# Six-tap gather and three-tap dense sampling: position rows broadcast by DMA through DRAM, the second corner sum moved to TensorE, V projected earlier

## What is computed

```python
feat = relu(norm_or_bias(conv1x1(x)))              # 64 channels, 32 x 32
off  = conv3x3(feat, w_off)                        # per pixel and tap: dy, dx (and a mask for b = 0)
py, px = y + ky + dy, x + kx + dx                  # where each of 9 taps samples
v    = sum over 4 corners of feat[corner] * weight(corner)   # bilinear
v    = v * sigmoid(mask)                           # b = 0 alone
out  = sum over taps of w2[tap] @ v[tap]           # 64 channels
x    = relu(x + conv1x1(norm_or_bias(out)))
```

## Time and profile before

| | |
|---|---|
| median of 3 runs (lowest, highest) | 242.6 us (241.63, 242.97) |
| the profiled execution, its span | 241.81 us, 240.0 us |
| busy: TensorE, VectorE, ScalarE, POOL | 190.2, 169.0, 112.0, 101.0 us |
| mean granted TensorE clock | 0.879 of full speed |

### The profile page before, as it was taken

How to read it: one execution, slowest core, us unless ns; L and a number is a source line. 1 busy time by engine, 2 the same in 40 slices (tenths; PEclk the granted TensorE clock), 3 DMA queues, 4 the chain that set the end, 5 groups by cost and what they waited for, 6 DMA issues and landing times. The chain is left out here.

```text
span 240.0 us, 2575 instructions
## 1 busy us (share of the span) xinstructions
PE 190.2 (79%) x894; PEld 104.7 (44%) x894; DVE 169.0 (70%) x276; ACT 112.0 (47%) x163; POOL 101.0 (42%) x111
## 2 busy tenths in 40 slices
PE   8998998866876878877977989386889878799920
PEld 7363958653322233333963668252233323243600
DVE  1996614599579889998375425997798999921272
ACT  2121304474885877641104422859559765124222
POOL 5000007787777777300000037777777775000010
PEclk9999997555799799999999995589599999999965
DMA  7500022323333333200000203323323333000004
GB/s 244 214 0 3 0 87 66 111 90 102 100 106 102 94 103 104 80 0 1 3 0 0 87 24 110 102 94 109 104 96 110 104 100 103 0 0 3 0 0 175
DMA packets 7887, 17.60 MB, mean 73 GB/s; under 512 B 1729, under 2 KB 3906, under 8 KB 7746
## 3 DMA queue, kind: packets, MB, share of 16 engines
q0 software_dynamic: 4608, 12.59, 16.8%
q1 hardware_dynamic: 3122, 4.32, 5.1%
q10 hardware_dynamic: 144, 0.52, 0.5%
HBM read 15.33 MB, written 2.10 MB: 73 GB/s over the span
## 5 line engine op out<-in xcount | busy, mean ns | idle before, releaser
L349 POOL DMA_INDIRECT G<-table,idx x96 | 95.0, 989 | 53.8 <-issue 42.9
L752 ACT ACTIVATE ps<-pos_y,second 128x1024 f32<-128x1024 f32 x48 | 52.7, 1113 | 13.8 <-DVE S L559 5.9
L336 POOL TENSOR_TENSOR rstd<-var,half_neg 128x1 f32<-128x1 f32 (+1 forms) x4 | 2.6, 638 | 76.5 <-DVE var L399 47.7
L572 DVE TENSOR_TENSOR GW<-G,ps 128x1024 f32<-128x1024 f32 (+1 forms) x32 | 30.3, 947 | 0.1
L559 DVE SCALAR_TENSOR_TENSOR x<-ps,hat_x 128x1024 f32<-128x1024 f32 x24 | 29.2, 1216 | 0.9 <-ACT ps L752 0.9
L983 PE MATMUL ps<-first,GS 128*128 128x128 f32 x48 | 12.9, 325 | 19.4 <-DVE GS L587 19.3
L824 PE MATMUL ps<-first 128*128 128x128 f32 x180 | 27.1, 305 | 0.0
L925 PE MATMUL ps<-om_split,sel 128*128 128x512 f32 x30 | 16.7, 597 | 12.5 <-ACT pos_y L732 4.7
L824 PEld LDWEIGHTS ps<-first 128*128 128x128 f32 x180 | 24.5, 214 | 4.0 <-issue 3.8
L939 PE MATMUL ps<-x,V 128*64 128x512 f32 x96 | 26.2, 624 | 0.0
L779 ACT ACTIVATE sT<-ps 128x256 f32<-128x256 f32 (+1 forms) x32 | 10.3, 321 | 24.2 <-PE ps L983 24.1
(11 more groups left out here) (135 smaller groups left out, 252.6 us busy)
## 6 DMA issues: line engine op xcount, KB each, us to landing
G<-table,idx POOLq DMA_INDIRECT x96, 2.7
second<-in_second SPq DMA_DIRECT2D x1, 1432.5 KB, 8.1
table<-feat_t SPq DMA_DIRECT2D x4, 256.0 KB, 2.2
out<-x SPq DMA_DIRECT2D x4, 256.0 KB, 2.2
x<-in_x ACTq DMA_DIRECT2D x1, 512.0 KB, 4.4
x<-in_x SPq DMA_DIRECT2D x1, 512.0 KB, 5.1
first<-in_first SPq DMA_DIRECT2D x1, 224.0 KB, 4.2
at_w<-in_w_b SPq DMA_DIRECT2D x1, 1.0 KB
```

The lines of the kernel that those rows point to most:

```text
L349: pool.indirect_dma_start(out=G[:, done % RING, k, :], out_offset=None, in_=table[b], in_offset=bass.IndirectOffsetOnAxis(ap=idx[b][:, n:n ...
L572: dve.tensor_tensor(GW[:, :, k0:k1].rearrange("p c k e -> p k c e"), G[:, (b * TILES + t) % RING, k0:k1].rearrange("p k (c e) -> p k c e", ...
L752: act.activation(near(cd), pos_y[:, (b * DENSE + i) % 2], ACT.Abs, bias=fld["own"][:, 1 + t:2 + t]).then_inc(s_ny, 1)
```

## The change

Positions (and the modulation after a sigmoid) of the three dense taps are picked out as rows by two products (`to_rows`), copied by ScalarE, written to a small DRAM tensor `row_table` by the SP queue, and read back nine times (six for b = 1) by DMAs that repeat one row of 4 KB over all 128 partitions into `hat_x`, `pos_y` and `mod_x`. `om_split`, `sel`, `near_x` and the `positions` products are gone, and ScalarE makes the x hat in place. VectorE stops after `GA`, which is now double buffered; TensorE adds the two halves of `GA` while it turns them, by accumulating two products with the identity. `V` is projected half before the offset convolution and half behind it, and `VS` comes from a product summed over tiles in PSUM.

```diff
+                sp.wait_ge(s_rows, b + 1)
+                for h in range(2):
+                    sp.dma_start(half(row_table[b][0:2 * DENSE], h),
+                                 places_r[h * HID:h * HID + 2 * DENSE]).then_inc(s_rowd[b], 16)
+                if b == 0:
+                    sp.wait_ge(s_masks, 1)
...
+                sp.wait_ge(s_rowd[b], 64 if b == 0 else 32)
+                for i in range(DENSE):
+                    for axis, dst in enumerate((hat_x[:, i], pos_y[:, i], mod_x[i])[:3 - b]):
+                        r = axis * DENSE + i
+                        sp.dma_start(dst, row_table[b][r:r + 1].to_broadcast([P, N])
+                                     ).then_inc(s_spread[b][i][axis], 16)
...
-                    dve.tensor_tensor(GA[:, :, k0:k1], GW[:, 0:2, k0:k1], GW[:, 2:4, k0:k1],
+                    if done >= 4:
+                        dve.wait_ge(s_st, done - 3)
+                    both = GW1 if part else GW0
+                    dve.tensor_tensor(GA[:, t % 2, :, k0:k1], both[:, 0:2], both[:, 2:4],
                                       ALU.add).then_inc(s_ga, 1)
                     for c in chunks:
                         product(c)
-                    dve.wait_ge(s_ga, done + 1)
-                    if done >= 4:
-                        dve.wait_ge(s_st, done - 3)
-                    dve.tensor_tensor(GS[:, t % 2, k0:k1], GA[:, 0, k0:k1], GA[:, 1, k0:k1],
-                                      ALU.add).then_inc(s_gs, 1)
...
             def prepare_x(b, i):
+                act.wait_ge(s_spread[b][i][0], 16)
+                act.activation(hat_x[:, i], hat_x[:, i], ACT.Abs, bias=fld["own"][:, 0:1]).then_inc(s_nx, 1)
+                act.wait_ge(s_nx, b * DENSE + i + 1)
+                act.activation(hat_x[:, i], hat_x[:, i], ACT.Relu, scale=-1.0, bias=1.0).then_inc(s_hx, 1)
...
-                keep_clock(7, IDLE[10 + b])
+                project(b, dense_weights, 0)
                 pe.wait_ge(s_offw, b + 1)
...
+                pe.wait_ge(s_ftD, b + 1)
+                to_rows(0)
+                project(b, dense_weights, 1)
+                to_rows(1)
                 to_pixels(1)
...
+                for t in range(TILES):
+                    mm = pe.matmul(ps[:, B_VS, 0:DENSE * HID], feat[:, t * P:(t + 1) * P], dense_weights[0:HID],
+                                   start=(t == 0), stop=(t == TILES - 1))
+                mm.then_inc(s_V, 1)
...
-                    for q in pairs(u):
-                        mm = pe.transpose(ps[:, B_ST, q * P:(q + 1) * P],
-                                          GS[:, t % 2, 2 * q:2 * q + 2, :].rearrange("p k e -> p (k e)"), ident)
+                    for n, q in enumerate(pairs(u)):
+                        for a in range(2):
+                            mm = pe.matmul(ps[:, B_ST[part], n * P:(n + 1) * P],
+                                           GA[:, t % 2, a, 2 * q:2 * q + 2].rearrange("p k e -> p (k e)"), ident,
+                                           start=(a == 0), stop=(a == 1))
```

More of the change, by code:

```diff
@@ L48 @@
 TAP_ENDS = [[sum(BESIDE[:u + 1]) >= n * TILES for u in range(UNITS)].index(True) for n in (1, 2)]
-PREPARE = [(-1, -1, -1)] + [(end - AHEAD - 2, end - AHEAD, end - AHEAD - 1) for end in TAP_ENDS]
+PREPARE = [-1] + [end - AHEAD - 2 for end in TAP_ENDS]
 NRING = 2
@@ L67 @@
          ("w2m", GROUPS0), ("w3c", HID), ("w3m", GROUPS0), ("ident", P)]
-SECOND = [("g2", P), ("g8", P), ("own", 1 + TILES), ("sel", 3 * DENSE), ("ramp", 2 * W), ("pick", PICK),
+SECOND = [("g2", P), ("g8", P), ("own", 1 + TILES), ("rows", HID), ("ramp", 2 * W), ("pick", PICK),
           ("b1w1", CT * HID), ("b1off", (TAPS + 1) * OM), ("b1w2", PAIRS * HID), ("b1wd", DENSE * HID), ("b1w3", C),
@@ L80 @@
 B_OM = 2
-B_ST = 2
-B_FILL = 1
+B_ST = [1, 2]
 B_CW = 3
+B_ROWS = 0
 B_NEAR = 4
@@ L156, in conv_chain @@
         VS = sb("VS", [P, DENSE, HID])
-        near_x = sb("near_x", [P, N])
-        w2bd = (near_x[:, 0:TAPS * HID]
+        hat_x = sb("hat_x", [P, DENSE, N])
+        pos_y = sb("pos_y", [P, DENSE, N])
+        w2bd = (pos_y[:, 0, 0:TAPS * HID]
                 .rearrange("p (t g o) -> p t g o", t=TAPS, g=GROUPS0))
-        hat_x = sb("hat_x", [P, DENSE, N])
-        mod_x = m0
-        pos_y = sb("pos_y", [P, 2, N])
+        mod_more = sb("mod", [P, DENSE - 1, N])
+        mod_x = [m0[:]] + [mod_more[:, i] for i in range(DENSE - 1)]
+        places_r = sb("places_r", [P, HALF])
+        masks_r = sb("masks_r", [P, HALF])
         S_own = sb("S", [P, N])
@@ L266, in chunks_at @@
             return range(sum(BESIDE[:u]), sum(BESIDE[:u + 1]))
-        def prepared_at(u, b):
-            return [(i, axis) for i in range(DENSE) for axis in range(3 - b)
-                    if PREPARE[i][axis] == u]
         def pixels_om(h):
@@ L542, in modulate @@
                 dve.wait_ge(s_hx, i + 1)
-                for h in range(2):
-                    dve.wait_ge(s_free[h], fill(0, i, 2) + 1)
-                dve.tensor_tensor(hat_x[:, i], hat_x[:, i], mod_x[:], ALU.mult).then_inc(s_hxm, 1)
+                dve.wait_ge(s_spread[0][i][2], 16)
+                dve.tensor_tensor(hat_x[:, i], hat_x[:, i], mod_x[i], ALU.mult).then_inc(s_hxm, 1)
                 dve.wait_ge(s_hxm, i + 1)
@@ L747, in chunk @@
                 if t == 0:
-                    for h in range(2):
-                        act.wait_ge(s_free[h], fill(b, i, 1) + 1)
+                    act.wait_ge(s_spread[b][i][1], 16)
+                if c == 0:
+                    act.wait_ge(s_weigh, 4 * b + 4)
                 if cd >= NRING:
                     act.wait_ge(s_S, cd - NRING + 1)
-                act.activation(near(cd), pos_y[:, (b * DENSE + i) % 2], ACT.Abs,
+                act.activation(near(cd), pos_y[:, i], ACT.Abs,
                                bias=fld["own"][:, 1 + t:2 + t]).then_inc(s_ny, 1)
@@ L849, in group_stats, with project, features @@
                           start=True, stop=True).then_inc(s_gm, 1)
-            def features(b):
+            def project(b, dense_weights, n):
+                if n == 1:
+                    pe.wait_ge(s_ftA, b + 1)
+                for t in range(4 * n, 4 * n + 4):
+                    mm = pe.matmul(ps[:, B_V[n], t % 4 * P:(t % 4 + 1) * P], feat[:, t * P:(t + 1) * P],
+                                   dense_weights[0:HID, 0:2 * HID], start=True, stop=True)
+                mm.then_inc(s_V, 1)
+            def features(b, dense_weights):
                 for t in range(TILES):
@@ L873, in to_pixels, with to_rows @@
                     om.then_inc(s_om, 1)
+                def to_rows(h):
+                    pe.wait_ge(s_omA, 2 * b + h + 1)
+                    pe.matmul(ps[h * HID:(h + 1) * HID, B_ROWS, :], fld["rows"][0:2 * SLOT], half(om_sb, h),
+                              start=True, stop=True).then_inc(s_rowm, 1)
                 for h in range(2):
@@ L1098, in constants @@
     own[:, 1:] = -(p // W)[:, None] - ROWS * np.arange(TILES)
-    sel = np.zeros((P, DENSE, 3), np.float32)
+    rows = np.zeros((P, HID), np.float32)
     for i in range(DENSE):
-        for axis in range(3):
-            sel[np.arange(4) * SLOT + axis * TAPS + GTAPS + i, i, axis] = 1
+        for axis, column in enumerate((i, DENSE + i, SLOT + i)):
+            rows[np.arange(2) * SLOT + axis * TAPS + GTAPS + i, column] = 1
     pick = np.zeros((P, PICK), np.float32)
@@ L1112, in constants @@
             "g8": np.kron(np.eye(P // 8), np.full((8, 8), 1 / 8)).astype(np.float32),
-            "own": own, "sel": sel, "pick": pick, "ramp": ramp}
+            "own": own, "rows": rows, "pick": pick, "ramp": ramp}
 def pack(fields, parts):
```

172 lines of the change are left out of this document (51 added, 121 removed).

## The result

| | before | after |
|---|---|---|
| median of the runs compared (lowest, highest) | 242.12 us (241.25, 242.97), 4 runs | 231.66 us (231.44, 232.78), 4 runs |
| ratio after to before | | 0.9578, 95% interval 0.9528 to 0.9627 |
| profiled execution | 241.81 us | 231.58 us |

The account below looks back on a forecast made before the run. VectorE was taken to bound both stages, with the gather stream as the floor. Stage 0 gives -8.0 and stage 1 -5.7: 241.8 - 13.7 = 228.1, and 0.8 for the median makes 228.9 us; range 225 to 236.

Parts of the forecast that it names:

- Stage b = 0, forecast -8.0: First stage: VectorE's loop starts at 50.4, takes 53.5 plus 1.0 idle, ends at 104.9 instead of 113.15, less 0.2.
- the 47 that was to prove that the clock held: Sign at VectorE's loop start in b = 0: a start at 47 instead of 50 to 51 means TensorE kept full clock.
- 0.2 back for two products in place of one transpose in the last unit: End of stage b = 0: the last unit's products on TensorE cost 0.2 us more than its transpose.
- Stage b = 1, forecast -5.7: Second stage: gathers set the end, `last_conv3` begins 6.2 us earlier, less 0.5 for later gathers.
- multiply and add 1.9, 203.5; four products 1.0, 204.5: End of b = 1: after the third last gather lands at 201.6, VectorE takes 1.9 us, TensorE's products 1.0.
- the data bind: Stage b = 1: VectorE alone would end at 203.4, so the landing of the last gathers sets the end.
- VectorE's predicted waits for gathers in the last units of b = 1: Sign at the end of b = 1: VectorE waits for gathers there for the first time.
- The last block, forecast 0: Block behind the two stages: the sum held no term for any change in its time.
- one 128x128 product 0.24: TensorE in each stage: 48 products at 0.24 us make 11.7 us, against 5.3 for 24 transposes.
- The rival built on four: TensorE bounds the stages at half clock or fourfold product cost: 20 us more per stage, 255 to 280; chance 0.06.
- The prediction is wrong if a product waits for `mod_x` or `hat_x`: Sign in VectorE's loop: any multiplication waiting for a position or modulation row read by DMA refutes the forecast.
- the third rival: Row reads delay the gather stream by 8 us in stage 0 and 5 in stage 1: 236 to 242 us; chance 0.09.

Follow-up runs that it names:

- e2: The changed kernel with the second corner sum back on VectorE and transposes on TensorE; ratio 0.9726 to the kernel before.
- e3: The changed kernel, but in the last tile of each stage (units 14 and 15) VectorE adds the second sum and TensorE transposes; 229.49 us, ratio 0.9492.
- e5: The changed kernel without the residual products of b = 1, so the output lacks that residual; 228.12 us, ratio 0.9404.
- e8: e3 with the last dense chunk moved one unit earlier; 229.52 us, ratio 0.9451 to the kernel before.
- e12: The same kernel as e8, run again in more rounds; 230.25 us, ratio 0.9472 to the kernel before.
- e9: e8 with the copy of VS behind the first unit of corners, reads not spaced; 230.37 us, ratio 0.9544.
- e11: e9 with all four residual products of b = 1 in unit 14; 229.77 us, ratio 0.9476 to the kernel before.
- e7: e6 with the copy of VS behind the first unit of corners, so VectorE's loop starts earlier; 230.48 us, ratio 0.9441.
- e4: The changed kernel with each x and y row read twice, first into a tile nobody reads; 238.49 us, ratio 0.9794.
- e1: The kernel before with only the second corner sum moved to TensorE; 241.14 us, ratio 0.9966.
- e10: The changed kernel with both projection halves and the idle products back where they stood before; 235.37 us, ratio 0.9767.
- e6: The changed kernel with row reads spaced: second tap's after the first's landed, third's after the fifth product; 233.09 us, ratio 0.9568.

## Why the prediction was right, and where it was off

**The bound.** Right: VectorE bound both stages, and its lag behind the gathers was what could be won. After the change it is idle for 0.9 us in the b = 0 loop, and its last `GA` ends at 102.61, 2.5 us behind the last gather's landing (issued at 97.27, and 2.8 from issue to landing) instead of 12.5. One reading was too simple: of TensorE's 8.5 us of idle time before the position products the row names 7.0 for ScalarE, and the other 1.5 were a wait for VectorE's sum into `VS`.

**Stage b = 0, forecast -8.0, measured -8.6.** The loop started at 48.78, not 50.4. The step that was off took the products for `V2` and `VS` at the slow pace: `V2` ran in 2.07 us, which is the full-clock price given beside it, and `VS` in 5.43, the low-clock price (5.0 forecast, scaled from a row that began at full clock: 38 to 40 us before had a grant of 0.64). The start is between the 50 to 51 that was forecast and the 47 that was to prove that the clock held; the grant was 1.00 up to 42 us, nearly to the end of `V2`, and 0.56 in 42 to 44. TensorE, before the loop:

```profile
40.49 2.07 PE L877 MATMUL ps<-second,feat 64*128 64x64 f32 x16
42.35 5.43 PE L881 MATMUL ps<-second,feat 64*128 64x192 f32 x16
```

From start to end the loop took 53.8 us, where 53.5 + 1.0 was forecast. The end at 102.61 is 0.4 before the 103 to 106 that was named. Against that, "0.2 back for two products in place of one transpose in the last unit" measured 1.9 us (tail 1.33 to 3.24): it priced the last unit's products alone, and left out that those of the unit before stand in the same queue ahead of them. e2 and e3, whose tails are 1.33 and 1.35 again, show that the products with the identity in the last units are the cause.

**Stage b = 1, forecast -5.7, measured -3.0.** `GA` of unit 14 was forecast 62.4 us after the stage's first gather, and is complete 195.40 - 132.96 = 62.44 after it. That agreement is in part luck. The gathers were 0.9 us quicker (the third last was issued 56.9 us after the first, 57.8 before), so the corners of unit 14 had landed by about 192.7 (189.86 and the median of 2.8), and VectorE took them up at 193.47 with no wait: it was still behind the data by 0.8 us. Its loop lasted 50.9 us, the 49.3 of the forecast and 1.5 us of waits that the sum did not hold.

The gathers started 0.45 us later relative to the stage before, forecast 0.5. The step that failed is the next: "multiply and add 1.9, 203.5; four products 1.0, 204.5". It let the products follow their data at once. They started 2.60 us later, since TensorE still had the last dense chunk, residual products and a contraction in its queue. That is the 2.7 us; what came behind took 4.25 us, where 1.0 + 1.9 + 1.3 = 4.2 was forecast. The sum held one group of residual products and not the one ahead of unit 14, though the earlier trace rows show the transposes of before starting at 210.73, 1.5 us after their sum.

So "the data bind" held for neither engine: VectorE's list bound unit 14, and TensorE's the end of the stage. e5 shows it by taking the residual out (0.9404 against 0.9578), and e8 and e12 by shortening what stands there: tails 4.3 and less, and 1.1 to 1.3% of the kernel. All four kernels with these edits (e8, e9, e11, e12) lie at 0.945 to 0.954; e9's interval reaches the change's. VectorE's predicted waits for gathers in the last units of b = 1 did not appear in the change, where it waited once, for 0.8 us, early in the stage; they appear in e7, e8, e9, e11 and e12, whose end is closer to the gathers.

**The last block, forecast 0, measured +1.4.** The products with `th` are no part of the change. TensorE's timeline has them before and after as:

```profile
225.83 3.69 PE L1082 MATMUL ps<-th,at_w 17*128 17x512 f32 x8
```

```profile
214.19 5.13 PE L1038 MATMUL ps<-th,at_w 17*128 17x512 f32 x8
```

The windows of this place after the change (columns as in the earlier trace rows) show the granted clock falling:

```profile
215.00:217.00 2.00, 2.00 (x5) 0.89 (x4) 1.40 (x2) 0.00 (x0) 0.00 (x0) 0.83 0.00 0
217.00:219.00 2.00, 2.00 (x3) 0.33 (x1) 0.70 (x1) 0.00 (x0) 0.00 (x0) 0.50 0.00 0
```

In the other profiles these products took 3.7 us (e3, e4, e8, e9, e11, e12), 4.0 to 4.4 (e5 to e7), or 5.2 to 6.3 (e1, e2, e10), none of which edits this place. All five kernels with the last tile's sum on VectorE have 3.7 and reach the block earliest, but so have e4 and the kernel before, which reach it late, so nothing here shows what sets the fall of the clock. It is a term that the forecast put at nothing and could not know from one profile. In the profiled executions the three terms leave the forecast 3.5 us short (0.6 more, 2.7 and 1.4 less); the medians differ by 2.8.

**TensorE.** The step "one 128x128 product 0.24" gave 11.7 us for a stage; the group of b = 0, 48 to 106 us, measures 16.0:

```profile
L939 PE MATMUL ps<-first,GA 128*128 128x128 f32 x96 | 16.0, 307 | 8.3 <-DVE GA L575 8.0
```

A unit's four products take 1.16 us and two 0.71. By my estimate from these two times a product takes 0.23 us and each group 0.26 more; the price had been taken from a row of 24 records in sequence, which pays that once. In the loop it did no harm: VectorE never waited for TensorE there, which was busy 51.3 of 60 us (forecast 48 of 54):

```profile
47.00:107.00 60.00, 51.26 (x282) 30.00 (x281) 54.67 (x65) 37.15 (x46) 39.58 (x40) 0.93 0.47 162
```

At the tail it is part of the 1.9. The rule of the Trainium skill ("TensorE: Matmul & The Clock Gate", Terms) that a transpose is four times faster for FP32 is not borne out at this size: two transposes 0.44 us, the four products that replace them 1.16, a factor of 2.6 with twice the instructions. Without the fixed part of a group the factor is larger, by an estimate from the same rows: one more transpose costs 0.11 us (0.44 less 0.33) and one more product 0.23, a factor of 2 for each instruction. The rival built on four is out: it needs over 64 us of TensorE work in a stage, and the kernel became faster.

**The rows.** The forecast had the first read at 46.7 to 49.6, the third at 51 to 54, 2.2 us each. Issued from 43.21 on, the first three landed 4.6, 5.9 and 7.6 us after their issue, at 47.8, 49.5 and 51.7, and the ninth at 64.2: on average one each 2.05 us. The x row of tap 0 was there at 47.8, before the 50 that was named, and VectorE waited 0.4 us for the third. "The prediction is wrong if a product waits for `mod_x` or `hat_x`" was its own mark, and this multiplication did wait for `mod_x`, if for 0.4 us, inside the 1.0 of idle time that was allowed. There is no slack: the same wait is 1.1 us in e3's profile and 2.1 in e5's. While the rows move, the DMA engines are full:

```profile
51.00:54.00 3.00, 3.00 (x15) 3.00 (x15) 2.56 (x3) 1.49 (x3) 2.47 (x2) 0.50 1.04 399
```

against a share of 0.25 before; the 320 GB/s that the prediction scaled from that share was low. The gathers land after a median of 6.5 us in 44 to 60. That mark, more than 4 us while rows move, was said to support the third rival, and was the wrong one: POOL went on issuing each 1.25 us, VectorE did not wait for a gather in b = 0 and for 0.8 us in b = 1, and e6 showed no price. The Trainium skill ("DMA: Bandwidth & Descriptors", Issuing engines are not separate DMA queues) says that DMAs started by the scalar, sync or gpsimd engine run on the same 16 and interleave; these rows agree, with gathers at 6.5 us instead of 2.7. Whether anybody waits is another question.

**What stays open.** How much of e9's distance from e7 is the contention seen in its trace was not measured. The fall of the clock to 0.50 between 38 and 44 us comes earlier or later from run to run, with the loop's start between 48.7 and 51.7 in kernels that keep the early projection and `VS` ahead of it (52.7 in e10), and no experiment separated that from the edits.

## What to carry to other kernels

A sum that moves from the bound engine to an in-order one can be free in the loop (here beside the rows, less so alone in e1) and is paid at the end of the stage: price the last items by what stands in the taking engine's list when their data arrive, not by the chain of data. Give the last one or two items back to the engine that is idle there, and move fill-in work out of the units before (here about 1% on top of 4.2%). A part that frees the bound engine can be worth little until another part clears the waits that would take its place, so such parts are measured alone and together.

## What the runs showed of the hardware

- One 4 KB row in DRAM, read over all 128 partitions (512 KB), lands 4.6 us after its issue in b = 0 and 4.3 in b = 1; nine in one queue land one each 2.05 us on average, and reads queued behind do not slow the ones ahead (third read: 7.5 and 8.9 us with three under way in e6 and e7, 7.6 and 9.0 with nine in the change and e9). With the gathers beside them all engines together move 399 GB/s (51 to 54 us, above) and 393 at a share of 1.0:

```profile
57.00:60.00 3.00, 3.00 (x18) 1.36 (x15) 2.48 (x4) 2.97 (x4) 2.39 (x3) 1.00 1.03 393
```

- Indirect gathers issued into that traffic land after 6.5 us instead of 2.7, while their issue keeps its pace, and VectorE waited for none of them in b = 0 of the change. In b = 1 it waited 0.8 us for one, and 3.4 in units 1 and 2 of e9, which starts its loop earlier.
- Small products have a fixed part in each group: 0.33 us for one 128x128 transpose, 0.44 for two, 0.71 for two products (four records), 1.16 for four products (eight records), and 2.92 for twelve in sequence.
- The same eight products with `th` took 3.69 to 6.25 us in different profiles; in the change's profile, with 5.13 us, the granted clock fell to 0.50 while they ran (windows above).
